# First layer of a four-layer graph network: first edges of a source found from TensorE's sums; 18 and 17 scatters in turn

## The chip, the cores and the metric

One Trainium2 chip, one core of it. The metric is the device time of one execution in microseconds (us); lower is better. TensorE is called PE (its weight loads PEld), VectorE DVE, ScalarE ACT, GpSimd POOL, SyncE SP.

## What is computed

Four graph layers run one after the other on 6250 nodes of 64 features and 206250 edges (100000 random pairs in both directions, and one loop for each node), sorted by destination. The change touches the first layer alone, and in it the mean of 48 edge features over the edges of each source:

```
def scatter_mean(src, index, dim_size):
    s = segment_sum(src, index, num_segments=dim_size)
    cnt = segment_sum(ones, index, num_segments=dim_size)
    return s / maximum(cnt, 1.0)[:, None]
edge_attr_agg = scatter_mean(edge_attr, edge_index[0], x.shape[0])
h = relu(concatenate([x, edge_attr_agg], axis=1) @ W1 + b1) @ W2 + b2
```

Each of the four layers is wrapped in layer normalisation, ReLU and a residual. The other three are a mean aggregation, an eight-head attention and a relational sum.

## The kernel before

The edges stand as 1612 columns of 128 (one edge on each partition). The first layer takes them in 62 halves of 26 columns (`HALF`); a loop of 31 rounds (`LOOPS`) holds two halves in its body, h = 0 and h = 1. Sources are random, so a source can occur several times in a column. Each half treats its columns in two ways.

The first 18 columns (`HS`) are scattered to tables in HBM. They go in five groups (`GROUPS`: four of four columns, one of two). For each group ACT copies the row of sources into PSUM (`rows`, L919). DVE then does two things: L849 compares each of the columns with its own sources, masked to the edges that stand earlier in the column (`lower`), and sums the result into `dups`; L853 makes `eq`, the full 128x128 equality matrix of each column. PE multiplies `eq` with the edge features and a one (`pack`, 49 columns; `sums`, L741), so that each edge holds the sum over all edges of its source in the column. ACT copies that to `val` (L950). An edge with an earlier one of the same source is sent to a dump row: DVE forms the row numbers in four small instructions (L862 to L870). POOL issues one indirect DMA for each column (L977) that adds 128 rows of `val` to one of four tables (`NACC`), taken in turn; a scatter waits for the landing of the one before it on its table, four scatters earlier.

The last 8 columns (`NZ`) never leave the core. DVE builds one-hot operands for a column (`spread`: one comparison L828 and three masked copies L831), and PE adds the column to sums that stay in PSUM for the whole loop (`z_add`, L748, 15 matmuls). The operands have two buffers, so a spread waits for the `z_add` two columns back. PE takes the work of a half as: sums 0, the histogram of the half before (`counts`, L724), z 0, sums 1, z 1, sums 2, z 2, sums 3, z 3, sums 4, z 4 to z 7. Sums k waits until ACT has copied sums k-1 out of the one bank that both use. DVE takes it as: group 0, spread 0, ..., group 3, spread 3, group 4, the four row-number instructions, spreads 4 to 7. ACT does, after each copy of sums, its part of the one-hot operands of the histogram (`hots`, L907 to L911), and between halves it copies the new features (L936) and splits them (L939, L941). Before the first copy of a half ACT waits (`s_vfree`) until POOL has got to the fourth scatter of the half before; before the first scatter of a half POOL waits for the row numbers (`s_tgt`) and for the last copy (`s_val`).

After the loop a chain of small steps on DVE, PE and SP (`tail0`, L470 to L598) must end, and all scatters must land, before the next stage starts.

Of the kernel before, what the change touches and what calls it, by code (L numbers as in the profile page):

```python
# [17 lines left out]
P = 128  # L18
# [24 lines left out]
HS = 18  # L43
NZ = HALF - HS
# [102 lines left out]
def build(nc, x, src, dst, edge_attr, edge_type, w0a, b0a, w0b, b0b, w1, b1, watt, att_s, att_d, batt, wf1, bf1, wf2,  # L147
# [57 lines left out]
    with top:  # L205
# [217 lines left out]

        GROUPS = [(r, min(r + 4, HS)) for r in range(0, HS, 4)]
        NG = len(GROUPS)
        assert NG % 2 and 2 * HS % NACC == 0
        W0 = FE + 1
        ZA = -(-J // ZB)
# [173 lines left out]
        with ExitStack() as ctx:  # L602
            attr = [sb(f"attr{h}", [P, HALF, FE], f32, ctx) for h in range(2)]
            pack = [sb(f"attr_and_one{h}", [P, HALF, FE + 1], f32, ctx) for h in range(2)]
            val = [sb(f"val{h}", [P, HS, D], f32, ctx) for h in range(2)]
            eq = [sb(f"eq{k}", [P, 4, P], f32, ctx) for k in range(2)]
            sfs = [sb(f"src_tile{h}", [P, HS], f32, ctx) for h in range(2)]
            dups = [sb(f"dups{h}", [P, HS], f32, ctx) for h in range(2)]
            scr = [sb(f"scratch{k}", [P, P], f32, ctx) for k in range(8)]
            tgt = sb("target_f", [P, HS], f32, ctx)  # L610
            ohlo = [sb(f"onehot_lo{h}", [P, HALF, P], bf16, ctx) for h in range(2)]
            ohhi = [sb(f"onehot_hi{h}", [P, HALF, HI], bf16, ctx) for h in range(2)]
            dig = [sb(f"src_digits{h}", [P, NZ, ZA + 1], f32, ctx) for h in range(2)]
            srow = [sb(f"src_rows{h}", [P, HS * P], f32, ctx) for h in range(2)]
# [17 lines left out]
            place0 = [borrow(0, ZA * P, bf16).rearrange("p (a c) -> p a c", c=P) for k in range(2)]  # L632
            left0 = [borrow(0, NZ * W0).rearrange("p (r f) -> p r f", f=W0) for n in range(2)]
            high0 = [borrow(1, NZ * W0, bf16).rearrange("p (r f) -> p r f", f=W0) for n in range(2)]
            HH = 2 * LOOPS
            digs = borrow(1, (HH + 1) * NZ * (ZA + 1))
            dig_v = digs[:, 0:HH * NZ * (ZA + 1)].rearrange("p (h r c) -> p h r c", r=NZ, c=ZA + 1)
            dig_i = borrow(1, HH * NZ, i32).rearrange("p (h r) -> p h r", r=NZ)
            dig_p, dig_j, dig_a = (borrow(1, HH * NZ).rearrange("p (h r) -> p h r", r=NZ) for n in range(3))
            src_z = src0f[:, 0:T].rearrange("p (h r) -> p h r", r=HALF)[:, :, HS:HALF]  # L640
# [9 lines left out]
            s_away, s_gap = (sem(f"l0_{n}", l0_sems) for n in ("digits_negated", "digit_distances"))  # L650
            s_srow = [sem(f"l0_src_rows_loaded{h}", l0_sems) for h in range(2)]
            s_turn, s_turnc, s_turnst = (sem(f"l0_{n}", l0_sems) for n in ("src_turned", "src_turned_copied", "src_turned_stored"))
            assert TT * P >= T + HALF > (TT - 1) * P and 12 < TT < 17 and TT * P <= HS * P
# [8 lines left out]
            with nc.Block() as block:  # L662
                @block.sync
                def _(e):
# [13 lines left out]
                    def load_rows(i, h):  # L678
                        hh = i * 2 + h
                        e.wait_ge(s_psrc, hh * NG + NG)  # L680
                        e.dma_start(srow[h][:, :], srct_d[bass.ds(hh * HALF * P, HS * P)].partition_broadcast(P))\
                         .then_inc(s_srow[h], 16)
# [24 lines left out]
                def _(e):  # L707
# [19 lines left out]
                    with e.Fori(0, LOOPS) as i:  # L727
                        for h in range(2):
# [3 lines left out]
                            def sums(k):  # L732
                                lo, hi = GROUPS[k]
# [4 lines left out]
                                for r in range(lo, hi):  # L738
                                    o = ps[6][:, (r - lo) * D:(r - lo + 1) * D]
                                    same_src = eq[(h + k) % 2][:, r - lo, :]  # L740
                                    last = e.matmul(o[:, 0:FE + 1], same_src, pack[h][:, r, :], start=True, stop=True)  # L741
                                last.then_inc(s_sum, 1)

                            def z_add(m):
                                e.wait_ge(s_spread, hh * NZ + m + 2)
                                for a in range(ZA):
                                    for n in range(SPLITS):
                                        last = e.matmul(ps[a][:, 0:ZW[a]], place0[(h * NZ + m) % 2][:, a, :],  # L748
                                                        spread0[(h * NZ + m) % 2][n].rearrange("p b f -> p (b f)")[:, 0:ZW[a]],
                                                        start=False, stop=False)  # L750
# [9 lines left out]
                            for m in range(NG - 1, NZ):  # L760
# [10 lines left out]
                def _(e):  # L771
                    e.tensor_copy(ps[7][:, 0:P], iota[:, :])
                    e.memset(digs[:, HH * NZ * (ZA + 1):(HH + 1) * NZ * (ZA + 1)], 0.0)
# [3 lines left out]
                    for h in range(2):  # L777
                        e.memset(val[h][:, :, FE + 1:D], 0.0)
                        last = e.memset(pack[h][:, :, FE:FE + 1], 1.0)
                    last.then_inc(s_init, 1)  # L780
# [7 lines left out]
                    e.tensor_scalar(dig_i, src_z, 21400.0, None, ALU.mult).then_inc(s_digits, 1)  # L788
# [5 lines left out]
                    e.scalar_tensor_tensor(dig_j, dig_p, -float(J), src_z, ALU.mult, ALU.add).then_inc(s_digits, 1)  # L794
# [8 lines left out]
                    for a in range(ZA):  # L803
                        e.scalar_tensor_tensor(dig_v[:, :, :, a], dig_a, float(a), dig_p, ALU.is_equal, ALU.mult)
                    e.scalar_tensor_tensor(dig_v[:, :, :, ZA], dig_a, -float(ZB), dig_j, ALU.mult, ALU.add)\
                     .then_inc(s_digits, 1)
                    e.wait_ge(s_digits, 9)
                    e.tensor_scalar(dig_v[:, :, :, 0:ZA].rearrange("p h r c -> p (h r) c"),
                                    dig_v[:, :, :, 0:ZA].rearrange("p h r c -> p (h r) c"), -1.0, None, ALU.add)\
                     .then_inc(s_digits, 1)  # L810

                    def rest_one(hh, h):
                        e.wait_ge(s_high, 2 * hh + 1)
                        e.wait_ge(s_spread, hh * NZ + 1)
                        e.tensor_tensor(left0[0], pack[h][:, HS:HALF, :], high0[0], ALU.subtract).then_inc(s_left, 1)

                    def rest_two(hh, h):
                        e.wait_ge(s_high, 2 * hh + 2)
                        e.wait_ge(s_left, 2 * hh + 3)
                        e.tensor_tensor(left0[1], left0[0], high0[1], ALU.subtract).then_inc(s_left, 1)  # L820

                    def spread(hh, h, m):
# [7 lines left out]
                        for n, t in enumerate((pack[h][:, HS + m, :], left0[0][:, m, :], left0[1][:, m, :])):  # L830
# [5 lines left out]
                    with e.Fori(0, LOOPS) as i:  # L836
                        for h in range(2):
# [3 lines left out]
                            for k, (lo, hi) in enumerate(GROUPS):  # L841
# [24 lines left out]
                            e.wait_ge(s_dup, hh * 3 + 2)  # L866
                            e.tensor_scalar(tgt[:, :], tgt[:, :], dumprow[:, 0:1], None, ALU.add).then_inc(s_dup, 1)
                            e.wait_ge(s_dup, hh * 3 + 3)
                            e.wait_ge(s_vfree, hh + 1)
                            e.tensor_copy(idx[h][:, 0:HS], tgt[:, :]).then_inc(s_tgt, 1)  # L870
# [2499 lines left out]
```

## Time and profile before

| | us |
|---|---|
| median of 3 runs | 7578.14 (7569.88 to 7579.32) |
| profiled execution, its own time | 7575.93 |
| its span, first to last instruction | 7574.1 |
| PE busy in the span | 6258.4 (83%) |
| DVE busy | 6223.6 (82%) |
| ACT busy | 4861.8 (64%) |
| POOL busy | 5347.8 (71%) |

The page gives shares over all four layers. The first layer's loop runs from 67 to 2131 us; only a view of that stretch tells what bounds it.

### The profile page before, as it was taken

Reading aid. Unit: us, or ns where it says so; the run is one execution under the profiler, and the core shown is the slowest. Engines: PE = TensorE matmul, PEld = TensorE weight load, DVE = VectorE, ACT = ScalarE, POOL = GpSimd, SP = SyncE. Lnnn points to the kernel's source line nnn. Section 1 sums busy time; section 2 is a strip of 40 time slices with the busy share of each in tenths; the row PEclk is TensorE's granted clock in tenths of the full one; section 3 lists DMA queues with packets and bytes.
Section 4 is the critical chain, followed back from the end, with each engine's and each line's share of the span. In section 5 each row is a group of like instructions: output and inputs, shape, how many; then the busy total and the mean of one; then the engine's idle time right before and its main releaser. Section 6 shows DMA issues by size and latency. Waiting matters only on the chain. (4 is left out here: it accounts for less than half of the span.)

```text
span 7574.1 us, 145887 instructions
## 1 busy us (share of the span) xinstructions
PE 6258.4 (83%) x38830; PEld 4411.6 (58%) x38831; DVE 6223.6 (82%) x16834; ACT 4861.8 (64%) x11241; POOL 5347.8 (71%) x4893
## 2 busy tenths in 40 slices
PE   6988888888867999975777777777777999999995
PEld 3545545544546888865666666666674544444443
DVE  7999999999969999957999999999986555555554
ACT  5777778778737888844555555555524677777773
POOL 4888888888865566657777777777513777777776
PEclk9999999999978999965666666666655999999997
DMA  5444444444431111124343444444331222222222
GB/s 130 75 75 72 69 75 72 69 75 72 66 74 39 24 24 24 24 53 63 64 65 64 64 65 64 65 64 65 55 93 47 65 76 70 70 70 76 70 70 55
DMA packets 626461, 487.11 MB, mean 64 GB/s; under 512 B 513289, under 2 KB 530030, under 8 KB 616344
## 3 DMA queue, kind: packets, MB, share of 16 engines
q0 software_dynamic: 281600, 185.95, 21.1%
q1 hardware_dynamic: 342455, 293.43, 13.3%
q10 hardware_dynamic: 2304, 6.55, 0.3%
q8 instruction: 41, 0.67, 0.0%
q14 instruction: 61, 0.50, 0.0%
HBM read 303.43 MB, written 182.13 MB: 64 GB/s over the span
## 5 line engine op out<-in xcount | busy, mean ns | idle before, releaser
L977 POOL DMA_INDIRECT acc<-val,idx x1116 | 1722.6, 1544 | 379.5 <-issue 320.4
L1601 POOL DMA_INDIRECT tile_rows<-att_row_table,src_by_tile x1620 | 1531.0, 945 | 502.9 <-issue 490.9
L748 PE MATMUL banks<-part 128*128 128x490 bf16 (+1 forms) x7440 | 1569.5, 366 | 218.8 <-DVE part L831 218.8
L3032 POOL DMA_INDIRECT rows_l<-relation_table,idx x1302 | 1245.7, 957 | 430.6 <-issue 386.4
L3237 PE MATMUL banks<-h_parts,dense_onehot 128*128 128x448 bf16 x6510 | 1316.2, 359 | 102.2 <-ACT dense_onehot L2985 99.7
L2270 PE MATMUL banks<-tile_rows,prob 128*128 x4032 | 854.1, 380 | 539.8 <-DVE kept_l L2368 538.7
L748 PEld LDWEIGHTS banks<-part 128*128 128x128 bf16 x7440 | 694.3, 97 | 996.7 <-DVE part L831 280.9
L2270 PEld LDWEIGHTS banks<-tile_rows,prob 128*128 128x128 f32 x4032 | 769.0, 285 | 638.0 <-issue 637.9
L3237 PEld LDWEIGHTS banks<-h_parts,dense_onehot 128*128 128x128 bf16 x6510 | 620.5, 99 | 730.0 <-issue 178.7
L907 ACT ACTIVATE digit_distance<-iota_row,dst_digits_negated 128x128 bf16<-128x128 f32 (+1 forms) x3224 | 868.7, 357 | 2.1 <-ACT dst_digits_negated L896 0.2
L1296 POOL DMA_INDIRECT gathered_rows<-h_table,gathered_index x600 | 579.4, 966 | 397.3 <-DMA gathered_rows<-h_table,gathered_index 245.7
L3149 DVE TENSOR_TENSOR h_nodes<-banks,dense_mask_j 128x448 f32<-128x448 f32 x310 | 192.9, 622 | 655.5 <-PE banks L3237 640.8
L831 DVE SCALAR_TENSOR_TENSOR part<-banks,src_digits,part 128x490 bf16<-128x490 f32 x992 | 671.8, 719 | 0.0
L1352 DVE TENSOR_SCALAR hot_code<-columns_bf,codes 128x196 bf16<-128x196 bf16 x2300 | 655.2, 289 | 0.0
L1351 DVE TENSOR_SCALAR hot_src_lo<-columns_bf,codes 128x128 bf16<-128x128 bf16 x2300 | 618.0, 271 | 32.7 <-ACT codes L1415 19.1
L2197 ACT ACTIVATE edge_logit<-banks 128x1024 f32<-128x1024 f32 x252 | 258.1, 1024 | 588.6 <-DVE banks L2319 586.3
L1454 ACT CAST counts<-banks 128x784 bf16<-128x784 f32 x650 | 525.9, 818 | 159.1 <-PE banks L1503 154.0
L2368 DVE SCALAR_TENSOR_TENSOR kept_l<-kept_l,fade,banks 128x65 f32<-128x65 f32 x2016 | 566.5, 281 | 59.4 <-PE banks L2270 5.3
L1528 PE MATMUL banks<-counts,h_parts 128*128 128x208 bf16 x4900 | 604.1, 268 | 0.0
L1528 PEld LDWEIGHTS banks<-counts,h_parts 128*128 128x128 bf16 x4900 | 480.0, 100 | 13.8
L2278 PE MATMUL banks<-ident,run 128*128 128x128 f32 x2016 | 481.6, 418 | 5.3 <-ACT fade L2205 5.3
L2211 ACT COPY prob<-banks 128x1024 f32<-128x1024 f32 x252 | 255.0, 1012 | 347.0 <-PE banks L2278 347.0
(449 smaller groups left out, 11835.1 us busy)
## 6 DMA issues: line engine op xcount, KB each, us to landing
src_rows<-src_by_column SPq DMA_DIRECT2D x63, 1152.0 KB, 5.9
piece_sums<-kept_l SPq DMA_DIRECT2D x252, 264.0 KB
running_sums<-run SPq DMA_DIRECT2D x62, 832.0 KB, 4.1
attr<-in_edge_attr SPq DMA_DIRECT2D x61, 624.0 KB
tile_rows<-att_row_table,src_by_tile POOLq DMA_INDIRECT x1620
rows_l<-relation_table,idx POOLq DMA_INDIRECT x1302
dense_code_rows<-src_by_column SPq DMA_DIRECT2D x62, 320.0 KB
acc<-val,idx POOLq DMA_INDIRECT x1116
```

What stands on the lines that cost most here:

```text
L748: last = e.matmul(ps[a][:, 0:ZW[a]], place0[(h * NZ + m) % 2][:, a, :], spread0[(h * NZ + m) % 2][n].rearrange("p b f -> p (b f)")[:, 0:ZW ...
L831: last = e.scalar_tensor_tensor(spread0[b][n], bc(ps[7][:, 0:ZB].unsqueeze(2), [P, ZB, W0]), dig[h][:, m, ZA:ZA + 1], bc(t.unsqueeze(1), [ ...
L907: last = e.activation(gap[n][:, r - a, :], iota[:, 0:w], ACT.Square, bias=away[n][:, r:r + 1])
L977: e.indirect_dma_start(acc_d[k], bass.IndirectOffsetOnAxis(ap=idx[h][:, r:r + 1], axis=0), val[h][:, r, :], None, compute_op=ALU.add).then ...
L1296: e.indirect_dma_start(grow[s][:, u, :], None, h1_d, bass.IndirectOffsetOnAxis(ap=gidx[s][:, u:u + 1], axis=0))\
L1351: e.tensor_scalar(hlo[slot(q)][:, u, :], cols[:, 0:P], code[s][:, 0, n:n + 1], None, ALU.is_equal)
L1352: last = e.tensor_scalar(hcd[slot(q)][:, u, :], cols[:, :], code[s][:, 1, n:n + 1], None, ALU.is_equal)
L1528: last = e.matmul(ps[4 + 1 - s][:, 0:BN * HT], parts4[:, m // 2, m % 2 * 2 * D:(m % 2 + 1) * 2 * D], table[1 - s][:, :, m // 2 * BN:(m // ...
L1601: e.indirect_dma_start(to, None, hx_d, bass.IndirectOffsetOnAxis(ap=src_col[:, t:t + 1], axis=0))\
L2270: last = e.matmul(summed(r), prob[u % 2][:, r, :], flat[:, bass.ds(cols[r], W1)], start=True, stop=True)
L3032: e.indirect_dma_start(g[h][:, r, :], None, y3_d, bass.IndirectOffsetOnAxis(ap=idx[h][:, r:r + 1], axis=0))\
L3237: last = e.matmul(ps[4 + b][:, 0:WJ], hot[h][:, k, m * P:(m + 1) * P], parts3[:, n, k * WJ:(k + 1) * WJ], start=(k == 0 and n == 0), stop= ...
```

## The change

The masked comparisons (L849) go. Two columns of weights are added to `pack`, so that PE's sums carry them: partition p holds 2^(62-2(p mod 64)) in the first of the two if p < 64 and in the second otherwise, and zero in the other. The sum of these weights over all edges of a source is below twice the weight of an edge only if that edge is the first one. The row numbers are now formed from `val`, after the last copy of a half, in five small instructions; spread 4 is moved ahead of them, and spreads 5 and on stay behind them. `HS` becomes 18 for the first half of a round and 17 for the second, `NZ` 8 and 9: one scatter less and one `z_add` more in a round. The tables are still taken in turn within a round of 35 scatters, so the first three scatters of a round follow the last on their table after three scatters, not four. The operands' buffer is chosen by the column's number in its half; spread 0 of h = 0 therefore waits for every `z_add` of the round before. Some ten small DVE instructions that make the weights come before the loop. The core of the diff:

```
-HS = 18
-NZ = HALF - HS
+HS = (18, 17)
+NZ = (HALF - HS[0], HALF - HS[1])
...
+        W2 = W0 + 2
...
-                                    last = e.matmul(o[:, 0:FE + 1], same_src, pack[h][:, r, :], start=True, stop=True)
+                                    last = e.matmul(o[:, 0:W2], same_src, pack[h][:, r, :], start=True, stop=True)
...
-                            for m in range(NG - 1, NZ):
+                            for m in range(NG - 1, NZ[h]):
                                 z_add(m)
...
+                    high, low, w = (rank[:, n:n + 1] for n in range(3))
+                    e.tensor_scalar(high, part_no[:, :], P // 2 - 0.5, None, ALU.is_gt).then_inc(s_rank, 1)
...
+                    for h in range(2):
+                        e.tensor_copy(pack[h][:, :, W0:W2], bc(rank[:, 3:5].unsqueeze(1), [P, HALF, 2]))
...
-                        e.wait_ge(s_z, hh * NZ + m + 1)
-                        b = (h * NZ + m) % 2
+                        e.wait_ge(s_z, z_count(i, h) + m + (2 if m == 0 and h == 0 else 1))
+                        b = m % 2
...
                                 e.wait_ge(s_sum, G + 2 * NG)
                                 e.wait_ge(s_eq, G + 1)
-                                for r in range(lo, hi):
-
-                                    e.scalar_tensor_tensor(scr[4 * m + r - lo][:, :], ps[5][:, (r - lo) * P:(r - lo + 1) * P],
-                                                           sfs[h][:, r:r + 1], lower[:, :], ALU.is_equal, ALU.mult,
-                                                           accum_out=dups[h][:, r:r + 1])
-
                                 e.tensor_tensor(eq[m][:, 0:n, :], ps[5][:, 0:n * P].rearrange("p (r j) -> p r j", j=P),
                                                 bc(sfs[h][:, lo:hi].unsqueeze(2), [P, n, P]), ALU.is_equal)\
                                  .then_inc(s_eq, 1)
...
-                            e.wait_ge(s_eq, (hh + 1) * NG + 2)
-                            e.tensor_scalar(dups[h][:, :], dups[h][:, :], 0.0, None, ALU.is_equal).then_inc(s_dup, 1)
-                            e.wait_ge(s_dup, hh * 3 + 1)
-                            e.scalar_tensor_tensor(tgt[:, :], sfs[h][:, :], dumprow[:, 0:1], dups[h][:, :],
+                            spread(hh, h, NG - 1)
+                            e.wait_ge(s_val, (hh + 1) * NG + 2)
+                            e.tensor_scalar(dups[h][:, :], val[h][:, :, W0], rank[:, 0:1], None, ALU.is_lt).then_inc(s_dup, 1)
+                            e.wait_ge(s_dup, hh * 4 + 1)
+                            e.scalar_tensor_tensor(dups[h][:, :], val[h][:, :, W0 + 1], rank[:, 1:2], dups[h][:, :], ALU.is_lt,
+                                                   ALU.mult).then_inc(s_dup, 1)
+                            e.wait_ge(s_dup, hh * 4 + 2)
+                            e.scalar_tensor_tensor(tgt[:, 0:HS[h]], sfs[h][:, :], dumprow[:, 0:1], dups[h][:, :],
                                                    ALU.subtract, ALU.mult).then_inc(s_dup, 1)
...
-                            e.tensor_copy(idx[h][:, 0:HS], tgt[:, :]).then_inc(s_tgt, 1)
-
-                            for m in range(NG - 1, NZ):
+                            e.tensor_copy(idx[h][:, 0:HS[h]], tgt[:, 0:HS[h]]).then_inc(s_tgt, 1)
+
+                            for m in range(NG, NZ[h]):
                                 spread(hh, h, m)
...
-                                e.copy(val[h][:, lo:hi, 0:FE + 1],
-                                       ps[6][:, 0:n * D].rearrange("p (u f) -> p u f", f=D)[:, :, 0:FE + 1])\
+                                e.copy(val[h][:, lo:hi, 0:W2],
+                                       ps[6][:, 0:n * D].rearrange("p (u f) -> p u f", f=D)[:, :, 0:W2])\
                                  .then_inc(s_val, 1)
...
-                            for r in range(HS):
-                                q, k = divmod(h * HS + r, NACC)
-
-                                e.wait_ge(s_add[k], (i * (2 * HS // NACC) + q) * 16 + 16)
+                            for r in range(HS[h]):
+                                q, k = divmod(h * HS[0] + r, NACC)
+
+                                e.wait_ge(s_add[k], (i * ADDS[k] + q) * 16 + 16)
```

`z_count(i, h)` is the number of columns given to `z_add` before that half; `ADDS[k]` is the number of scatters of a round that go to table k.

## Rows read from the trace of the kernel before

**Rows 1.** The page, the granted TensorE clock in 40 slices of the span.
```profile
PEclk9999999999978999965666666666655999999997
```

**Rows 2.** Busy time of each engine in one stretch of the first layer's loop.
```profile
200.00:2100.00 1900.00, 1696.76 (x10434) 953.77 (x10432) 1783.25 (x4522) 1482.28 (x4505) 1583.58 (x1028) 1.00 0.48 72
```

**Rows 3.** Waits: engine, line, waited for, us in total, times, longest us.
```profile
POOL acc L977 <- DMA acc<-val,idx: 22.2, 63, 1.3
...
ACT banks L919 <- POOLq L980: 193.6, 54, 4.0
...
PE banks L748 <- DVE part L831: 203.1, 285, 1.2
```

**Rows 4.** Timeline, POOL: start us, us, engine, line, operation, count, idle before.
```profile
1000.24 1.54 POOL L977 DMA_INDIRECT acc<-val,idx  x1 [0.30 <-issue]
1002.09 1.54 POOL L977 DMA_INDIRECT acc<-val,idx  x1 [0.30 <-issue]
...
1033.49 1.54 POOL L977 DMA_INDIRECT acc<-val,idx  x1 [0.30 <-issue]
...
2163.23 1.54 POOL L977 DMA_INDIRECT acc<-val,idx  x1 [0.30 <-issue]
```

**Rows 5.** Timeline, ACT: one half, from the release by POOL to the last copy.
```profile
1002.17 0.59 ACT L919 COPY banks<-src_rows 128x512 f32<-128x512 f32 x1 [3.61 <-POOLq L980]
1002.70 0.32 ACT L950 COPY val<-banks 128x196 f32<-128x196 f32 x1
...
1007.66 0.32 ACT L950 COPY val<-banks 128x196 f32<-128x196 f32 x1
...
1021.33 0.23 ACT L950 COPY val<-banks 128x98 f32<-128x98 f32 x1
```

**Rows 6.** Timeline, DVE: end of the groups of a half, the targets, two spreads.
```profile
1016.93 0.35 DVE L849 SCALAR_TENSOR_TENSOR scratch<-banks,src_tile,strict_lower 128x128 f32<-128x128 f32 x1
...
1017.48 0.42 DVE L853 TENSOR_TENSOR eq<-banks,src_tile 128x256 f32<-128x256 f32 x1
1017.93 0.18 DVE L862 TENSOR_SCALAR dups<-dups 128x18 f32<-128x18 f32 x1
...
1018.83 0.81 DVE L828 TENSOR_TENSOR part<-banks,src_digits 128x640 bf16<-128x640 f32 x1
...
1024.88 0.82 DVE L828 TENSOR_TENSOR part<-banks,src_digits 128x640 bf16<-128x640 f32 x1 [0.69 <-PE banks L748]
...
1026.26 1.35 DVE L831 SCALAR_TENSOR_TENSOR part<-banks,src_digits,part 128x490 bf16<-128x490 f32 x2
```

**Rows 7.** Timeline, TensorE: last one-hot sums of a half, first sums of the next.
```profile
1027.66 2.85 PEld L748 LDWEIGHTS banks<-part 128*128 128x128 bf16 x15 [0.21 <-DVE part L831]
...
1030.71 2.85 PEld L748 LDWEIGHTS banks<-part 128*128 128x128 bf16 x15 [0.20 <-DVE part L831]
...
1033.65 1.05 PEld L741 LDWEIGHTS banks<-attr_and_one,eq 128*128 128x128 f32 x8
1033.84 0.99 PE L741 MATMUL banks<-attr_and_one,eq 128*128 128x49 f32 x8
```

**Rows 8.** Busy time by engine, clock, DMA share, GB/s after the last scatter.
```profile
2140.00:2145.00 5.00, 0.77 (x3) 0.39 (x3) 1.44 (x8) 0.00 (x0) 4.08 (x4) 0.50 0.39 27
...
2166.00:2167.00 1.00, 0.25 (x4) 0.17 (x3) 0.62 (x3) 0.00 (x0) 0.00 (x0) 0.50 0.00 0
```

**Rows 9.** Timeline: the loop's first and last copy, and the stage's end.
```profile
67.40 0.59 ACT L919 COPY banks<-src_rows 128x512 f32<-128x512 f32 x1 [5.58 <-DMA src_rows<-src_by_column]
...
74.49 0.33 ACT L950 COPY val<-banks 128x196 f32<-128x196 f32 x1 [1.58 <-PE banks L741]
...
2100.51 0.32 ACT L950 COPY val<-banks 128x196 f32<-128x196 f32 x1
...
2131.43 0.91 PEld L724 LDWEIGHTS banks<-onehot_hi,onehot_lo 128*128 128x128 bf16 x26
...
2172.75 0.19 DVE L598 TENSOR_SCALAR quad_row<-quad_row_f 128x49 int32<-128x49 f32 x1 [4.59 <-DMA quad_row_f<-quad_row_of_node]
```

More of the change, by code:

```diff
@@ L422, in build @@
         c0.close()
-        GROUPS = [(r, min(r + 4, HS)) for r in range(0, HS, 4)]
-        NG = len(GROUPS)
-        assert NG % 2 and 2 * HS % NACC == 0
+        GROUPS = [[(r, min(r + 4, HS[h])) for r in range(0, HS[h], 4)] for h in range(2)]
+        NG = len(GROUPS[0])
+        ADDS = [len(range(k, NSL, NACC)) for k in range(NACC)]
+        assert NG % 2 and NG == len(GROUPS[1]) and HS[0] >= HS[1] and NZ[0] % 2 == 0
         W0 = FE + 1
+        W2 = W0 + 2
         ZA = -(-J // ZB)
@@ L631, in build, with of_half, z_count @@
             spread0 = [[borrow(0, ZB * W0, bf16).rearrange("p (b f) -> p b f", f=W0) for n in range(SPLITS)] for k in range(2)]
-            place0 = [borrow(0, ZA * P, bf16).rearrange("p (a c) -> p a c", c=P) for k in range(2)]
-            left0 = [borrow(0, NZ * W0).rearrange("p (r f) -> p r f", f=W0) for n in range(2)]
-            high0 = [borrow(1, NZ * W0, bf16).rearrange("p (r f) -> p r f", f=W0) for n in range(2)]
+            hots0 = borrow(0, ZA * P)
+            place0 = [hots0.bitcast(bf16)[:, k * ZA * P:(k + 1) * ZA * P].rearrange("p (a c) -> p a c", c=P) for k in range(2)]
+            left0 = [borrow(0, NZ[1] * W0).rearrange("p (r f) -> p r f", f=W0) for n in range(2)]
+            high0 = [borrow(1, NZ[1] * W0, bf16).rearrange("p (r f) -> p r f", f=W0) for n in range(2)]
             HH = 2 * LOOPS
[L636 to L640, printed above, removed]
+            NZT = LOOPS * NZL
+            digs = borrow(1, (NZT + NZ[0]) * (ZA + 1))
+            dig_v = digs[:, 0:NZT * (ZA + 1)].rearrange("p (t c) -> p t c", c=ZA + 1)
+            assert NZT <= ZA * P
+            dig_i = hots0[:, 0:NZT].bitcast(i32)
+            dig_p, dig_j, dig_a = (borrow(1, NZT) for n in range(3))
+            src_l = src0f[:, 0:T].rearrange("p (i r) -> p i r", r=2 * HALF)
+            src_z = [src_l[:, :, h * HALF + HS[h]:(h + 1) * HALF] for h in range(2)]
+            def of_half(t, h):
+                return t.rearrange("p (i r) -> p i r", r=NZL)[:, :, h * NZ[0]:h * NZ[0] + NZ[h]]
+            def z_count(i, h):
+                return i * NZL + h * NZ[0]
             l0_sems = []
@@ L649, in build @@
             s_init, s_tail, s_pack = (sem(f"l0_{n}", l0_sems) for n in ("init", "tail", "packed"))
-            s_away, s_gap = (sem(f"l0_{n}", l0_sems) for n in ("digits_negated", "digit_distances"))
+            s_away, s_gap, s_rank = (sem(f"l0_{n}", l0_sems) for n in ("digits_negated", "digit_distances", "rank"))
             s_srow = [sem(f"l0_src_rows_loaded{h}", l0_sems) for h in range(2)]
             s_turn, s_turnc, s_turnst = (sem(f"l0_{n}", l0_sems) for n in ("src_turned", "src_turned_copied", "src_turned_stored"))
-            assert TT * P >= T + HALF > (TT - 1) * P and 12 < TT < 17 and TT * P <= HS * P
+            assert TT * P >= T + HALF > (TT - 1) * P and 12 < TT < 17 and TT * P <= HS[0] * P
             def turned_tiles(b):
@@ L840, in _ @@
                             rest_one(hh, h)
-                            for k, (lo, hi) in enumerate(GROUPS):
+                            for k, (lo, hi) in enumerate(GROUPS[h]):
                                 G, n, m = hh * NG + k, hi - lo, (h + k) % 2
@@ L881, in _ @@
                     e.sem_inc(s_val, 2)
-                    e.copy(sfs[0][:, :], src0f[:, 0:HS]).then_inc(s_stage, 1)
+                    e.copy(sfs[0][:, :], src0f[:, 0:HS[0]]).then_inc(s_stage, 1)
                     for b in range(-(-TT // 4)):
@@ L932, in _ @@
                             e.wait_ge(s_tgt, hh + 2)
-                            e.copy(sfs[1 - h][:, :], src0f[:, bass.ds((hh + 1) * HALF, HS)]).then_inc(s_stage, 1)
+                            e.copy(sfs[1 - h][:, :], src0f[:, bass.ds((hh + 1) * HALF, HS[1 - h])]).then_inc(s_stage, 1)
                             e.wait_ge(s_attr[h], (i + 1) * 16)
@@ L938, in _ @@
                             e.wait_ge(s_left, 2 * hh + 1)
-                            e.copy(high0[0], pack[h][:, HS:HALF, :]).then_inc(s_high, 1)
+                            e.copy(high0[0][:, 0:NZ[h], :], pack[h][:, HS[h]:HALF, 0:W0]).then_inc(s_high, 1)
                             e.wait_ge(s_left, 2 * hh + 3)
-                            e.copy(high0[1], left0[0]).then_inc(s_high, 1)
+                            e.copy(high0[1][:, 0:NZ[h], :], left0[0][:, 0:NZ[h], :]).then_inc(s_high, 1)
                             e.wait_ge(s_vfree, hh + 1)
-                            for k, (lo, hi) in enumerate(GROUPS):
+                            for k, (lo, hi) in enumerate(GROUPS[h]):
                                 n = hi - lo
```

94 lines of the change are left out of this document (58 added, 36 removed).

## The prediction, made before the changed kernel ran

> **What bounds the kernel now.** The page's shares mix four layers, so I went straight to the first layer's loop. In 1900 us of it DVE is busy 1783 (94%), PE 1697 (89%), POOL 1584 (83%), ACT 1482 (78%) [rows 2]. By that DVE would be the bound and less DVE work the cure. The waits say otherwise. POOL, the least suspicious by share, starts a scatter every 1.847 us: 1000.24, 1002.09, and the first scatter of the next half at 1033.49, which is 33.25 us or 18 x 1.847 [rows 4]. The 0.30 us between two scatters is its own issue, and for landings it waits 22.2 us in 63 times, hardly more than those 0.30 each [rows 3]. ACT waits for POOL up to 4.0 us in each half [rows 3]: at 1002.17 it is let go by POOL after 3.61 us of idling, 1.9 us after POOL started the half before [rows 4, 5]. So POOL sets the pace, 62 x 33.25 us, and the others follow through that release.
>
> How much slower could POOL be overtaken? I take the ring that closes if POOL were no limit, counted from V0, the start of the first copy L950 of a half, to the next V0. ACT is in one unbroken chain from V0 to the fifth copy: 1002.70 to 1021.33, 18.63 us [rows 5]. DVE's row numbers are no part of it. PE's sums 0 for the next half end at 1034.83 [rows 7], 1.1 us before the next V0, which is at 1002.70 + 33.25 = 1035.95. So the ring of before takes about 32.1 us of the 33.25: close behind POOL.
>
> **The change part by part.**
>
> *Scatters.* One less in a round of two halves: 35 x 1.847 = 64.6 us instead of 66.5. That is POOL's new limit, 1.85 us a round or 57 us over 31 rounds if nothing else binds.
>
> *Masked comparisons gone.* Two of them take 1016.93 to 1017.48, 0.275 us each [rows 6]; 18 a half are 5.0 us of DVE. DVE is not the bound, so this is worth only what it shortens in the ring: `eq` is ready earlier, but ACT's chain up to the fifth copy does not wait for DVE, and stays 18.63 us.
>
> *The new wait.* DVE now waits for the fifth copy before it forms the row numbers, and spreads 5 to 7 (or 8) are queued behind that wait; PE's z 5 waits for spread 5, everything after on PE for z 5, the next sums 0 for the last z, and the next V0 for sums 0. That makes one serial ring through all of ACT's groups and then through PE's last `z_add`s. Its terms:
> - V0 to the fifth copy: 18.63 us [rows 5].
> - The copy 0.23 [rows 5], release of DVE about 0.1, and the small instructions: four took 1017.93 to 1018.83, 0.90 [rows 6]; five of the same kind 1.15. Together 1.50.
> - Spread 5: 1024.88 to 1027.61, and PE's load starts at 1027.66: 2.78 [rows 6, 7].
> - z 5, z 6, z 7: two of them run from 1027.66 to 1033.65, 3.00 each [rows 7]: 9.00. A half with nine adds z 8: 12.00.
> - Sums 0, from its first load to the end of its last matmul: 1033.65 to 1034.83, and 0.05 to the copy: 1.23 [rows 7].
>
> That is 33.14 us for a half with eight `z_add`s and 36.14 with nine. Spread 0 of h = 0 now also waits for the last z of the round before: from the end of that z, 0.12 + 2.78 + z 0 3.00 + sums 1 1.23 = 7.13 us to the second copy. The way by ACT is 1.23 + (1007.66 - 1002.70) = 6.19 [rows 5]. So that half grows by 0.94 to 34.08. A round takes 34.08 + 36.14 = 70.2 us, above POOL's 64.6 and above the 66.5 of before: +3.7 us a round. POOL idles some 5.6 us of each.
>
> The Trainium skill (TensorE: Matmul & The Clock Gate, Architectural detail) says that the queues of ScalarE and VectorE are strictly first in, first out. By that spreads 5 to 8 cannot pass the wait and a round is 70.2 us; if they could, it would be rival 2's 66.7. The trace of before has no such wait in that place and cannot show it.
>
> *What costs nothing.* Two more columns in 49: 4% of the sums' 0.99 us and of the copies' 0.32, under 0.1 us of a ring, 0 to 3 us in all; I take 0. The instructions for the weights, ten at about 0.2 us, lie ahead of 67.40, where ACT waits 5.58 us for a load of sources [rows 9]; that covers them, and without cover they cost 2 us. The shorter distance on a table at the start of a round: three scatters are 5.54 us. The last scatter of the loop starts at 2163.23, and no DMA moves between 2166 and 2167 [rows 4, 8], so its data were down in under 3.8 us; the one bound from above is that four scatters, 7.39 us, nearly always suffice [rows 3]. I take no wait; at worst 1.85 us a round, 57 us, which POOL's idling in my ring hides too.
>
> *Sum.* The first copy is at 74.49, that of the last half at 2100.51 [rows 9]. After: 74.5 + 30 rounds x 70.2 + one half 34.1 = 2214.6, 114 us later. Behind it, the end: z 7 was followed by `counts` at 2131.43, 30.9 us after the last V0 [rows 9]; now the last z ends 36.14 - 1.23 = 34.9 us after it, 4 us more. The same chain `tail0` then runs to 2172.75 [rows 9], and the scatters end long before it (fifth copy + 1.5 + 17 x 1.847 = 51.5 us after V0, against 76). The stage ends 118 us later. The profiled execution took 7575.9 us, 2.2 below the median of the runs shown, which is nothing: 7576 + 118 = **7694 us**. Against the median that is 1.5% slower.
>
> **The rivals.**
>
> 1. *POOL stays the bound* (faster). Then the wait for the fifth copy is hidden, as DVE has 5.0 us less to do and PE needs only eight or nine z of 3.00, five sums and the counts, about 61 us of the 64.6 of a round. The last V0 comes 30 x 1.85 = 55 us earlier, the last half is 4 us longer: 7576 - 51 = 7525 us. It decides if a round's ring is under 64.6, that is if my ring is 5.6 us too long. For it: ACT and DVE each had slack. Against it: that slack is in front of POOL's release and at the end of the spreads, and my ring uses neither. With a scatter landing later than 5.54 us it would shrink by as much as 57 us.
>
> 2. *Ring without the wait* (no change). DVE gets to the row numbers only when the fifth copy is there, or the wait hides. Then z 4 starts about 17.6 us after V0 (ACT's last rows, `eq`, spread 4), z 5 follows 3.8 later behind five small instructions and spread 5, and z 6, z 7, sums 0 as before: about 31.4 and 34.4 a half, 0.9 for spread 0: 66.7 us a round. 31 x 0.2 + 4 gives 7586 us, within 0.2%, about what a measurement of this kernel can tell from no change. Against it: spread 4 ends some 17.3 to 18.4 us after V0, the fifth copy 18.9 to 19.9. DVE is there before it.
>
> 3. *PE's clock falls.* PE now idles about 2.5 us between z 4 and z 5 in each half, where its longest wait in the loop was 1.2 us [rows 3]. The granted clock is 1.00 throughout the loop [rows 2], and 0.50 at 2140, where PE has 0.77 us of work in 5 [rows 8] and after; later slices of the page are at 5 and 6 tenths [rows 1]. If it were halved for z 5 alone, 3.0 us a half are added, 62 x 3.0 = 186: 7880 us. The Trainium skill (TensorE: Matmul & The Clock Gate, Part 1: The HAM clock gate) says that the slow level is the default and that sustained activity releases it; by that rule, and by the rows, the small idling here should leave it at full, as PE still has 61 us of work in 70.
>
> **How the numbers follow.** My forecast has 0.75, rival 1 0.12, rival 2 0.07, rival 3 0.06. Within the forecast, each release may be off by 0.05 us and there are about seven in a half; with the two columns and the first half that is 1 us a round, 31 us either way: 7660 to 7728. The range that holds 8 in 10 takes in a little of a partly hidden wait below and of a partly lowered clock above: 7645 to 7740. Slower by over 0.2%: 0.81; faster 0.12; same 0.07.
>
> **What would show it.** In the profile after: V0 to V0 34 and 36 us in turn; ACT no longer released by POOL at L919 but waiting for PE at the first copy; POOL idle 5 us a round before a half's first scatter; DVE idle before the small instructions, released by ACT's copy; PE idle 2.5 us before one z in each half, released by DVE; the second copy of h = 0 late by 1 us. I am wrong if scatters still follow each other at 1.847 us across halves (rival 1), if DVE doesn't idle before the row numbers (rival 2), or if the clock in the loop is below 1.00 (rival 3). A ring right in kind and wrong in size would show in the copies' times, term by term.

## The result, and the profile after

The changed kernel takes 7739.17 us (median of 5 runs, 7733.11 to 7741.16) against 7572.81 before in the same measurements: ratio 1.0216, 95% interval 1.0201 to 1.0231. It is slower by 166 us, where 118 were forecast; 7739.2 lies less than 1 us inside the upper edge of the range given, 7740. The span of the profiled execution is 7738.1 us, 164.0 more than before.

All of it is in the first layer's loop. Below is the timeline of ACT after, start and duration in us: the first copy of sums of three halves in a row (1007.02, 1041.22, 1078.91), and in the first of these halves the second and the fifth copy.

```profile
1007.02 0.33 ACT L986 COPY val<-banks 128x204 f32<-128x204 f32 x1 [2.38 <-PE banks L755]
...
1013.07 0.33 ACT L986 COPY val<-banks 128x204 f32<-128x204 f32 x1 [1.02 <-PE banks L755]
...
1026.78 0.23 ACT L986 COPY val<-banks 128x102 f32<-128x102 f32 x1
...
1041.22 0.33 ACT L986 COPY val<-banks 128x204 f32<-128x204 f32 x1 [2.33 <-PE banks L755]
...
1078.91 0.33 ACT L986 COPY val<-banks 128x204 f32<-128x204 f32 x1 [2.38 <-PE banks L755]
```

In [rows 5] ACT was let go by POOL and the next half came 33.25 us later. Here each first copy is released by PE's sums (L755), after 2.4 us of idling. The halves take 34.20 and 37.69 us. The second copy of h = 0 comes 6.05 us after the first, for want of PE; before it was 4.96 [rows 5]. The fifth is then 19.76 us behind the first: 18.6 and the late second copy.

Who waits for whom between 200 and 2200 us (engine, line, waited for, us in total, times, longest):

```profile
POOL acc L1013 <- DVE idx L906: 188.2, 28, 7.2
...
DVE dups L895 <- ACT val L986: 88.3, 55, 1.6
...
ACT val L986 <- PE banks L755: 160.4, 84, 2.4
...
PE banks L762 <- DVE part L869: 230.6, 194, 2.3
```

POOL, which before waited only the 22.2 us for landings [rows 3] beside its own issue, waits 188 us for the row numbers in 28 halves, 6.7 each: one half of every round. DVE waits for ACT's fifth copy 55 times; at 35.9 us a half the 2000 us hold about 56 halves, so it is every half that has the wait that the change put in. No line of ACT's is released by POOL any more; the 193.6 us of [rows 3] are gone. How the wait travels is seen in one half:

```profile
1025.48 2.80 PEld L762 LDWEIGHTS banks<-part 128*128 128x128 bf16 x15 [0.63 <-DVE part L869]
...
1027.05 0.24 DVE L895 TENSOR_SCALAR dups<-val,rank_weights 128x18 f32<-128x18 f32 x1 [1.62 <-ACT val L986]
...
1028.14 0.18 DVE L906 CAST idx<-target_f 128x18 int32<-128x18 f32 x1
...
1028.24 0.82 DVE L866 TENSOR_TENSOR part<-banks,src_digits 128x640 bf16<-128x640 f32 x1
...
1029.30 1.54 POOL L1013 DMA_INDIRECT acc<-val,idx  x1 [7.21 <-DVE idx L906]
...
1031.02 0.94 PEld L762 LDWEIGHTS banks<-part 128*128 128x128 bf16 x6 [2.74 <-DVE part L869]
```

PE loads for z 4 at 1025.48. DVE stands idle until 1027.05 for ACT's copy, forms the row numbers (1027.05 to 1028.24) and only then begins spread 5. PE has no operands before 1031.02, 2.74 us after its last load. (Between matmuls the gap is 2.3 us, the longest PE wait above; a matmul runs on a little after its load.) POOL starts its half at 1029.30 after 7.21 us of idling.

The busy time of the engines in stretches tells the rest (us, PE, PEld, DVE, ACT, POOL, granted clock, DMA):

```profile
200.00:2100.00 1900.00, 1679.91 (x9989) 919.22 (x9987) 1479.87 (x2438) 1380.73 (x4182) 1440.36 (x928) 0.98 0.44 66
...
1062.00:1063.00 1.00, 0.00 (x0) 0.00 (x0) 1.00 (x3) 1.00 (x5) 0.69 (x2) 1.00 0.00 0
1063.00:1064.00 1.00, 0.01 (x1) 0.02 (x2) 1.00 (x3) 0.97 (x3) 1.00 (x1) 1.00 0.61 33
1064.00:1068.00 4.00, 4.00 (x12) 1.59 (x13) 2.57 (x4) 2.24 (x5) 3.39 (x3) 0.57 0.42 56
```

Over these 1900 us DVE falls from 1783 us [rows 2] to 1480: it is less busy, in a slower kernel. The granted clock is 0.98, no longer 1.00. The other three rows show where it goes: PE does nothing in 1062 to 1063 and 0.01 us in the next, and in the 4 us after that the granted clock is 0.57, between the levels of 1.2 and 2.4 GHz. That loses (1 - 0.57) x 4 = 1.7 us. The clock's records show 28 such falls in the 31 rounds, 27 of them before the last half, and at most one in a round, though each of the 62 halves has a gap of this length before z 5. Most falls lie in the half with nine `z_add`s, which then takes 37.7 us; seven lie in the other, which then takes 35.8 instead of 34.2.

The end of the stage:

```profile
2259.57 0.33 ACT L986 COPY val<-banks 128x204 f32<-128x204 f32 x1 [2.33 <-PE banks L755]
...
2296.05 0.91 PEld L738 LDWEIGHTS banks<-onehot_hi,onehot_lo 128*128 128x128 bf16 x26
...
2336.45 0.19 DVE L602 TENSOR_SCALAR quad_row<-quad_row_f 128x49 int32<-128x49 f32 x1 [4.42 <-DMA quad_row_f<-quad_row_of_node]
```

The last half's first copy is 159.1 us later than in [rows 9], and the stage's end 163.7 us later. The 164.0 us of the span are all here.

### The profile page after: what moved, and what is told of

Same layout as the page of the kernel before. It is cut to its first block and busy times, and to the rows that moved or that the text cites. A ratio compares the mean times of both kernels' runs of the same rounds, so it can differ in the third digit from the quotient of the medians.

```text
span 7738.1 us, 144940 instructions
## 1 busy us (share of the span) xinstructions
PE 6389.7 (83%) x39233; PEld 4462.4 (58%) x39234; DVE 6020.5 (78%) x14802; ACT 4867.1 (63%) x11241; POOL 5307.8 (69%) x4862
## 5 line engine op out<-in xcount | busy, mean ns | idle before, releaser
L1013 POOL DMA_INDIRECT acc<-val,idx x1085 | 1684.3, 1552 | 565.5 <-issue 346.7
L762 PE MATMUL banks<-part 128*128 128x490 bf16 (+1 forms) x7905 | 1720.0, 373 | 255.8 <-DVE part L869 255.7
L762 PEld LDWEIGHTS banks<-part 128*128 128x128 bf16 x7905 | 757.1, 99 | 1119.3 <-DVE part L869 320.0
L869 DVE SCALAR_TENSOR_TENSOR part<-banks,src_digits,part 128x490 bf16<-128x490 f32 x1054 | 712.5, 717 | 0.0
L866 DVE TENSOR_TENSOR part<-banks,src_digits 128x640 bf16<-128x640 f32 x527 | 430.9, 818 | 145.5 <-PE banks L762 144.3
```

What stands on the lines that cost most here:

```text
L762: last = e.matmul(ps[a][:, 0:ZW[a]], place0[m % 2][:, a, :], spread0[m % 2][n].rearrange("p b f -> p (b f)")[:, 0:ZW[a]], start=False, sto ...
L869: last = e.scalar_tensor_tensor(spread0[b][n], bc(ps[7][:, 0:ZB].unsqueeze(2), [P, ZB, W0]), dig[h][:, m, ZA:ZA + 1], bc(t.unsqueeze(1), [ ...
L1013: e.indirect_dma_start(acc_d[k], bass.IndirectOffsetOnAxis(ap=idx[h][:, r:r + 1], axis=0), val[h][:, r, :], None, compute_op=ALU.add).then ...
```

## The experiments

Each time is a median with a run of the kernel before beside it on the same chip; experiments are compared by their ratios to it, as it moved between 7565 and 7573 us. The lengths of halves below are taken between the first copies of sums (the line that is L986 in the changed kernel) of successive halves. A "round" is two halves: 66.5 us before, 71.9 us after with the fall of the clock. "The loop's row" is the row of the windows for 200 to 2100 us, in the columns named above.

**1. One more spread ahead of the wait.**

```
+                            spread(hh, h, NG)
                             e.wait_ge(s_val, (hh + 1) * NG + 2)
...
-                            for m in range(NG, NZ[h]):
+                            for m in range(NG + 1, NZ[h]):
```

> One more spread (5) moved ahead of the row numbers, nothing else. Theory (the serial ring through ACT's fifth copy, five small instructions and spread 5, and on top a short fall of PE's clock in the gap that this makes): with spread 5 ready in time the gap before z 5 goes, halves take 32.0 and 34.0 us (66.0 a round), the clock stays at 1.00, the kernel takes about 7563 us. If the clock still falls once a round, 1.7 us a round more: 7615. Rival (the ninth z_add and the two-buffer wait are what costs, the new wait is hidden): little moves, 7700 to 7740.

Measured: 7568.82 us, ratio 0.9998 (0.9988 to 1.0007). One spread moved gives back all 166 us. ACT's first copies of three halves, and the second of the first:

```profile
1002.14 0.33 ACT L987 COPY val<-banks 128x204 f32<-128x204 f32 x1 [2.37 <-PE banks L755]
...
1008.19 0.33 ACT L987 COPY val<-banks 128x204 f32<-128x204 f32 x1 [1.00 <-PE banks L755]
...
1034.57 0.33 ACT L987 COPY val<-banks 128x204 f32<-128x204 f32 x1 [2.68 <-PE banks L755]
...
1068.54 0.33 ACT L987 COPY val<-banks 128x204 f32<-128x204 f32 x1 [2.37 <-PE banks L755]
```

32.43 (0.4 more than expected) and 33.97 us. PE waits for operands 217 times between 200 and 2000 us, 123.8 us in all. The longest wait is 1.3 us instead of 2.3, and the clock never falls in the loop. The second copy is still 6.05 us behind the first. So it was the wait's place in DVE's queue, not DVE's work, that cost the time.

**2. PE kept busy in the gap.** The rest is the changed kernel's.

```
                                 z_add(m)
+                                if m == NG - 1:
+                                    e.wait_ge(s_val, (hh + 1) * NG + 2)
+                                    for n in range(16):
+                                        e.matmul(ps[6][:, 256:512], ohlo[1 - h][:, n, :], ..., start=True, stop=True)
```

> 16 matmuls of 256 columns (about 1.7 us of PE work) whose result nobody reads are put between z 4 and z 5, where PE idles 2.5 us; all else as in the changed kernel. Theory (each round one stretch of 3.4 us at half clock, because of that idle gap, costs 1.65 us): the granted clock stays at 1.00 in the loop, the halves take 34.2 and 36.0 in every round, and the kernel takes 7694 us. Rival (the clock falls for the load as a whole or for another gap, or the difference of rounds has another cause): 37.7 remains in most rounds and the time is 7740 or a little more.

Measured: 7694.79 us, ratio 1.0164 (1.0147 to 1.0181), within 1 us of the time of the theory and of my forecast. (The forecast stood on 7576 us for the kernel before; beside this run it took 7572.6, so the difference is 122 us where 118 were forecast.) ACT's first copies of three halves, in the timeline:

```profile
1021.38 0.33 ACT L991 COPY val<-banks 128x204 f32<-128x204 f32 x1 [2.33 <-PE banks L755]
...
1057.40 0.33 ACT L991 COPY val<-banks 128x204 f32<-128x204 f32 x1 [2.38 <-PE banks L755]
...
1091.62 0.33 ACT L991 COPY val<-banks 128x204 f32<-128x204 f32 x1 [2.32 <-PE banks L755]
```

The halves here take 36.02 and 34.22: the 37.7 are gone. PE's timeline at one such place, the loads behind the filling, from z 5 on:

```profile
1011.19 4.83 PEld L762 LDWEIGHTS banks<-part 128*128 128x128 bf16 x25 [0.84 <-DVE part L874]
```

The loop's row:

```profile
200.00:2100.00 1900.00, 1769.93 (x11063) 1011.97 (x11062) 1511.72 (x2491) 1412.82 (x4274) 1470.15 (x947) 1.00 0.44 68
```

The gap is 0.84 us and the clock 1.00. 1.7 us of useless work in each half make the kernel 44 us faster. The last half's first copy is at 2215.3, 44.3 us sooner than in the changed kernel: all of it is in the loop.

**3. No wait, same instructions.** The five instructions stand where they stood, but read the feature tile.

```
-                            e.wait_ge(s_val, (hh + 1) * NG + 2)
-                            e.tensor_scalar(dups[h][:, :], val[h][:, :, W0], rank[:, 0:1], None, ALU.is_lt)
+                            e.tensor_scalar(dups[h][:, :], pack[h][:, 0:HS[h], W0], rank[:, 0:1], None, ALU.is_lt)
...
```

> The row numbers are formed by the same five small instructions in the same place, but from the weights in the feature tile instead of the copied sums, so that DVE has nothing to wait for; every edge goes to its dump row, so the sums of the scattered columns are lost. Theory: without the wait a half takes 31.4 and a half with nine z_adds 34.4, plus 0.9 for spread 0: 66.7 a round, about 7586 us, and no fall of the clock if PE's gap before z 5 is under 1 us. Rival (the five instructions and the order of the spreads cost it, not the wait): 7690 to 7740.

Measured: 7600.95 us, ratio 1.0039 (1.0025 to 1.0053); halves of mostly 32.6 and 34.4, 67.2 a round over the whole loop, clock 1.00. The wait costs 138 us of the 166, fall of the clock included; the ninth z_add, the wait of spread 0 and the new order keep 28. The time is 15 us above the expected one, and 0.5 us more in each of 31 rounds is all of it. The expected halves were added up wrongly: the terms of rival 2 (17.6 + 3.8 + 9.0 + 1.23) make 31.6 and 34.6, not 31.4 and 34.4, and with 0.9 for spread 0 that is 67.2 a round. The scatters that all go to dump rows land later (POOL waits 70.9 us for landings between 200 and 2000, against 8 to 22 in the other runs' loops), but no half is held by it: every first copy is released by PE, none by POOL.

**4. Eight and nine z_adds by themselves.** Comparisons and row numbers as before the change, 18 and 17 scatters in turn.

```
+                                for r in range(lo, hi):
+                                    e.scalar_tensor_tensor(scr[4 * m + r - lo][:, :], ..., lower[:, :], ALU.is_equal, ALU.mult,
+                                                           accum_out=dups[h][:, r:r + 1])
...
-                            spread(hh, h, NG - 1)
-                            e.wait_ge(s_val, (hh + 1) * NG + 2)
+                            e.wait_ge(s_eq, (hh + 1) * NG + 2)
```

> The masked comparisons and the old place of the row numbers are kept (they are formed from them, before spread 4, with no wait); only the 18 and 17 scatters in turn stay, with eight and nine z_adds. Theory (behind POOL's 33.25 us lies a ring of 32.1, and a ninth z_add adds 3.0 to every second): the halves take 32.5 and 35.1, 67.6 a round, about 7612 us: the scatter saved gains nothing by itself. Rival (POOL is the bound, and one scatter less in a round is worth 1.85 us): 64.6 a round, about 7525 us.

Measured: 7656.36 us, ratio 1.0113 (1.0096 to 1.0130). Right in kind (the scatter saved gains nothing, the ring of the others is longer), 44 us off in size: 33.3 and 35.6, 68.9 a round. ACT in this run between 200 and 2000 us:

```profile
ACT banks L956 <- DVE eq L890: 59.5, 52, 1.2
```

The copy of the next group's sources waits for `eq` in every half, 1.14 us each. But this wait does not end last. In one half it is over at 1000.64 (V0, the first copy, is at 1002.47), and what it releases, the comparisons of group 1, starts only at 1003.81, because DVE makes spread 0 first. z 0 then loads 0.95 us late, sums 1 stand behind it, and the second copy is at 1008.05, 5.58 us after the first, not 4.97:

```profile
1000.64 0.59 ACT L956 COPY banks<-src_rows 128x512 f32<-128x512 f32 x1 [1.13 <-DVE eq L890]
...
1003.81 0.35 DVE L887 SCALAR_TENSOR_TENSOR scratch<-banks,src_tile,strict_lower 128x128 f32<-128x128 f32 x1
...
1003.95 2.80 PEld L763 LDWEIGHTS banks<-part 128*128 128x128 bf16 x15 [0.95 <-DVE part L870]
...
1006.84 1.05 PEld L756 LDWEIGHTS banks<-attr_and_one,eq 128*128 128x128 f32 x8
```

None of this is new. The kernel before does the same at its start, while POOL is not yet behind:

```profile
107.80 0.33 ACT L950 COPY val<-banks 128x196 f32<-128x196 f32 x1 [1.29 <-PE banks L741]
...
113.27 0.33 ACT L950 COPY val<-banks 128x196 f32<-128x196 f32 x1 [0.44 <-PE banks L741]
...
138.74 0.59 ACT L919 COPY banks<-src_rows 128x512 f32<-128x512 f32 x1 [1.17 <-DVE eq L853]
140.62 0.33 ACT L950 COPY val<-banks 128x196 f32<-128x196 f32 x1 [1.29 <-PE banks L741]
```

There the first copies are released by PE, the second comes 5.47 us later, and the seven halves from 107.80 to 337.18 take 32.8 us each. So the ring behind POOL was 32.8 us, not 32.1. That is what the expectation lacked, and the wait of spread 0 for the last `z_add`.

**5. The same with a third operand buffer for the ninth column**, so that spread 0 of the next round waits for no z_add of the last.

```
-                        b = m % 2
+                        b = 2 if m == 8 else m % 2
...
-                        e.wait_ge(s_z, z_count(i, h) + m + (2 if m == 0 and h == 0 else 1))
+                        e.wait_ge(s_z, z_count(i, h) + m + 1)
```

> e5_turn with the third buffer for the ninth column. e5_turn took 68.9 us a round where I had 67.6; I had left the wait of spread 0 for the last z_add out of its ring. If that is the missing term, the second copy of h = 0 comes 5.0 us after the first instead of 6.06 and a round takes 68.0: about 7628 us. Rival (another wait of DVE's longer queue is what I missed): 68.9 remains, 7656 us.

Measured: 7628.27 us, ratio 1.0086 (1.0070 to 1.0103). The time is the expected one, the way to it only in part: a round takes 68.3 us, and the second copy comes 5.49 us after the first (5.57 in the other half), not 5.0. Spread 0's wait for the last z_add was 0.6 us a round of the missing 1.3. The rest goes to the rival, DVE's queue: the halves are 32.8 and 35.4, the ring of before and the same with 2.6 more, where 32.5 and 35.1 were put.

**6. 18 scatters in both halves**, all else changed. With eight columns in each half the two buffers come in turn again, and spread 0 waits for the `z_add` two columns back only.

```
-HS = (18, 17)
+HS = (18, 18)
...
-                        e.wait_ge(s_z, z_count(i, h) + m + (2 if m == 0 and h == 0 else 1))
+                        e.wait_ge(s_z, z_count(i, h) + m + 1)
```

> The changed kernel with 18 scatters and eight z_adds in both halves: only the weights, the new wait and the order of the spreads are left of the change. Ring of 33.1 to 33.3 us against POOL's 33.25, so 66.5 a round. If PE's clock falls for the idle gap before z 5, which is still there, 1.7 us a round come on top in most rounds: 68.1 a round, about 7620 us. If it needs the ninth z_add and the longer ring, the clock stays at 1.00 and the time is that of before, 7573 to 7578 us. Rival (the new wait costs nothing here since POOL paces it): 7573 us with ACT released by POOL in each half.

Measured: 7629.22 us, ratio 1.0080 (1.0065 to 1.0096). The halves take 33.4 or, with a fall of the clock, 34.8. The loop's row:

```profile
200.00:2100.00 1900.00, 1692.70 (x10157) 934.42 (x10154) 1487.59 (x2449) 1449.70 (x4391) 1560.48 (x1003) 0.97 0.46 70
```

The clock is 0.97. So the fall needs neither the ninth z_add nor the long ring; it goes with the gap. And even where the ring alone, 33.4 us, all but fits POOL's 33.25, the wait costs 59 us. Most of that are the falls: 33 of them in the loop, 1.4 us each, make 46.

**7. Spread 5 ahead and the third buffer.** The edits of 1 and 5 together.

> As e1_ahead, and the ninth column of a half gets a third buffer of its own, so that spread 0 of the next round doesn't wait for the last z_add. Theory: the second copy of h = 0 comes 4.96 us after the first, not 6.06, and the half is 0.9 to 1.0 us shorter: 31.5 and 34.0, 65.5 a round, about 7541 us. Rival (that wait is hidden, e.g. behind ACT or the next wait for spread 3): 66.4 as in e1_ahead, 7569 us.

Measured: 7529.55 us, ratio 0.9947 (0.9932 to 0.9962), 31.1 and 34.0 us, 65.1 a round: 11 us better than expected, most of it in the half with eight z_adds (31.5 expected). The second copy is back at 4.98 us. Of the versions here this is the first that is faster than the kernel before.

**8. Spread 4 ahead of the last group's comparison, spread 5 ahead of the row numbers.**

```
                             for k, (lo, hi) in enumerate(GROUPS[h]):
+                                if k == NG - 1:
+                                    spread(hh, h, NG - 1)
...
-                            spread(hh, h, NG - 1)
+                            spread(hh, h, NG)
                             e.wait_ge(s_val, (hh + 1) * NG + 2)
...
-                            for m in range(NG, NZ[h]):
+                            for m in range(NG + 1, NZ[h]):
```

> Two spreads moved: spread 4 ahead of group 4's comparison (DVE idles there for ACT's copy of the sources), spread 5 ahead of the row numbers. Theory: PE's waits for spreads 4 and 5 shrink, the ring falls to about 64.4, POOL is the bound again with 35 x 1.847 = 64.6 us a round: about 7523 us, ACT released by POOL in one half of two. Rival (the ring keeps its length because something else of it, ACT's chain or sums 4, ends last): 66.4 a round, 7569 us.

Measured: 7526.29 us, ratio 0.9942 (0.9929 to 0.9956), 31.4 and 33.6, 65.0 a round. The time is close to the expected 7523; that POOL is the bound again is true of few halves, as the next experiment shows.

**9. Both, 7 and 8.**

> e7_two_ahead with the third buffer of e6_ahead_third. If e7_two_ahead is bound by POOL, nothing more comes: 64.6 a round, 7523 us. If it is still bound by the ring (65 or more a round), up to 0.9 us a round less, and then 64.6 a round.

Measured: 7525.81 us, ratio 0.9940 (0.9926 to 0.9953). The two cannot be told apart by time. ACT's wait for POOL's release in the waits of experiment 8, without the third buffer:

```profile
ACT banks L957 <- POOLq L1018: 27.5, 12, 4.1
```

And in those of this one, with it:

```profile
ACT banks L960 <- POOLq L1021: 163.2, 55, 5.5
```

Twelve releases in 1800 us against 55, 27.5 us against 163.2: with the third buffer POOL releases ACT in every half again, as in [rows 3], now with 35 scatters a round. That is rival 1's time, 7525 us, reached with two places changed in DVE's queue and a third buffer; experiment 8 comes as near with the places alone. (Against the kernel before beside it, it is 45 us faster, where rival 1 had 51.)

**10. The order of 8 with 18 scatters in both halves.**

> The order of e7_two_ahead with 18 scatters and eight z_adds in both halves. Theory (with the short ring POOL is the bound, so the scatter left out in a round is all of the gain over before): 66.5 a round as before, ACT released by POOL in each half, clock 1.00, about 7570 us, the time of before. Rival (the shorter work of DVE or the new order gains by itself): 7525 to 7550 us.

Measured: 7576.12 us, ratio 1.0016 (1.0007 to 1.0026). Without the scatter left out there is no gain; the kernel is even 11 us slower. Between 200 and 2100 us ACT waits for POOL, more than ever:

```profile
ACT banks L957 <- POOLq L1018: 343.6, 57, 6.8
```

But the clock does fall here, which I had not expected. Timeline, first a row of ACT and then two of PE, in one half:

```profile
1035.62 0.59 ACT L957 COPY banks<-src_rows 128x512 f32<-128x512 f32 x1 [6.16 <-POOLq L1018]
...
1036.98 0.97 PEld L755 LDWEIGHTS banks<-attr_and_one,eq 128*128 128x128 f32 x8 [0.88 <-DVE eq L887]
...
1039.62 0.11 PEld L762 LDWEIGHTS banks<-part 128*128 128x128 bf16 x2 [1.67 <-DVE part L869]
```

The loop's row, and that of a stretch behind the gap:

```profile
200.00:2100.00 1900.00, 1732.26 (x10312) 939.95 (x10310) 1507.29 (x2502) 1482.37 (x4502) 1587.83 (x1023) 0.97 0.47 72
...
1040.00:1044.00 4.00, 4.00 (x14) 1.51 (x13) 2.71 (x5) 4.00 (x15) 3.39 (x3) 0.60 0.31 18
```

ACT idles 6.16 us for POOL, PE meanwhile finds nothing for 0.88 us, has one set of sums, and then nothing for 1.67 us; in the 4 us after 1040 the clock is 0.60. Such a fall loses 1.6 us of PE's time. There are 31 of them in the loop, 50 us in all, and the kernel is 11 us slower than before, so most of that lies beside POOL's pace. Whether the 11 us are theirs is not shown.

## Why the prediction was right, and where it was short

*What bounds.* POOL's 33.25 us a half with a ring close behind: right. But the ring was 32.8 us, not 32.1 (experiment 4): the sum had ACT's chain alone between the first copy and the second, 4.97 us, where DVE's queue and z 0 make it 5.47 as soon as POOL does not hold the first copy back. The forecast for the changed kernel did not suffer, since without the comparisons DVE is sooner at spread 0 and the second copy of the nine-`z_add` half is back at 4.98 us. Experiment 10 and the kernel before take the same time to 0.2% with some 5 us less of DVE work in a half ((1783 - 1507) / 57).

*The queue.* Spread 5 started at 1028.24, behind the row numbers, though its operands did not need them. Experiment 1 shows that this order is what costs. The rule of the Trainium skill that the forecast named (TensorE: Matmul & The Clock Gate, Architectural detail: VectorE's queue is first in, first out) agrees with that 1028.24.

*The ring.* Its terms came out as put: the half with eight z_adds 34.20 us (34.08), the one with nine 36.02 where the clock does not fall in it and in every round of experiment 2 (36.14), the second copy 1.09 us late (0.94), PE's gap 2.3 to 2.7 us (2.5), DVE's wait before the row numbers 1.6. Experiments 1 and 3 take the wait away in two ways and get 166 and 138 us back.

*Where the sum was short.* The last V0 was put at 2214.6 and came at 2259.6. The missing 45.0 us are the clock: 27 falls before it of 37.69 - 36.02 = 1.67 us; with the gap filled (experiment 2) it comes at 2215.3. That the measured time still lies in the range is luck: the uncertainty that was worked out, 31 us either way, ends at 7728, and the 12 us above it that just hold 7739.2 were allowed for a partly lowered clock without a price. This was rival 3, to which I gave 0.06. Its cause, the idle gap before z 5, was right: experiment 2 shows it, in which filling the gap alone brings 7694.8 us. Both its chance and its size were wrong: I priced a fall for z 5 of each half, 62 x 3.0 us, where there is at most one in a round and it costs 1.67. And I took "PE is busy 61 us of 70" as a reason for a steady clock. The busy share of the loop does not tell the two apart: it is 88% in the changed kernel (1680 of 1900 us) and was 89% before. The Trainium skill (TensorE: Matmul & The Clock Gate, Part 1: The HAM clock gate) says that sustained activity releases the slow level. I read it as leaving the clock at full over so small an idling; the 0.57 granted behind the gap refutes that reading.

*The end.* 4 us were forecast for the longer last half, 4.6 measured (163.7 - 159.1), though the 28th fall lies in it: `counts` starts 36.5 us after the last V0, 5.6 later than before, and the chain behind it makes up 1.0. The start, the two extra columns and the shorter distance between scatters of one table cost nothing that can be seen: the first copy comes at 73.9 (74.5 before), and POOL waits 15.3 us in all for landings between 200 and 2200 us.

*Rival 1* fell, but only for this order of DVE's queue: experiment 9 reaches its 7525 us. *Rival 2* was close to what experiment 3 does (7586 forecast, 7601 measured), which is the same ring without the wait; its own terms add up to about 7600.

Not settled: why the clock falls after 28 of 62 gaps of one length and not after the others (in 21 rounds in the half with nine z_adds, in seven in the other, in three in neither); and why the half with eight z_adds in experiment 7 is some 0.4 us better than worked out.

## What to carry to other kernels

When work is taken off the busiest engine, ask first which engine paces the loop; here it was POOL, third by its share of busy time, and while it did, 5 us a half less for DVE were worth nothing (experiment 10). Then ask how close the next bound is, and look for stretches of the trace in which it shows itself: the first halves of the loop had the ring's 32.8 us to read off. A wait costs what is queued behind it: before putting one into an in-order queue, put ahead of it as many of the independent instructions as the next engine needs to stay busy while the wait lasts; here one spread was worth 166 us. And close the ring: if the awaited result comes at the end of another engine's chain, and that chain's next start hangs on what is behind the wait, the times add up.

## What the runs showed of the hardware

The changed kernel has a gap in PE's work in every half, 2.3 us between matmuls and 2.7 between loads, in a loop in which PE is busy to 88%. After 28 of these 62 gaps a stretch followed that was partly at 1.2 GHz (0.57 granted over 4 us), which costs 1.7 us; after the others the clock stayed at 2.4 GHz. Between 200 and 2000 us, waits of 1.3 us at most were followed by no fall in experiments 1, 3, 7 and 8. In experiment 10 two loads' gaps of 0.88 and 1.67 us, with one set of sums between them, were followed by one. Of the 57 halves there that have the gap of 1.67 us, 31 have a fall. Sixteen matmuls in the gap whose result nobody reads kept the clock at 2.4 GHz and made the kernel 44 us faster.
